# The loop over the attention slots written out in every engine's program

## The reference, cut to what matters

```python
x = x + xattn(layernorm(x), ctx, ctx, mask, Wq, bq, Wk, bk, Wv, bv, Wo, bo)   # 16 heads of 8
x = x + ffn(layernorm(x), Wr, W1, b1, W2, b2)                                 # 8 experts, top 2

# xattn: q = qn @ Wq + bq, k = c @ Wk + bk, v = c @ Wv + bv, per head
score = q @ k.T / sqrt(8); attn = softmax(score); out = (attn @ v) @ Wo + bo
# ffn: probs = softmax(x @ Wr.T); each token goes to its best two experts
h = gelu(x @ W1[e] + b1[e]); y = h @ W2[e] + b2[e]
```

## Time and profile before

| what | value |
|---|---|
| median of three runs | 1009.66 us (1009.06 to 1009.77) |
| the profiled execution, its own time | 1012.47 us |
| its span, first to last instruction | 1010.7 us |
| mean granted TensorE clock | 0.915 |
| PE / DVE / ACT / POOL busy | 81% / 70% / 54% / 49% |
| instructions in the trace | 22541 |

### The profile page before, as it was taken

How to read it: one execution, slowest core, us unless ns; L and a number is a source line. 1 busy time by engine, 2 the same in 40 slices (tenths; PEclk the granted TensorE clock), 3 DMA queues, 4 the chain that set the end, 5 groups by cost and what they waited for, 6 DMA issues and landing times.

```text
span 1010.7 us, 22541 instructions
## 1 busy us (share of the span) xinstructions
PE 822.4 (81%) x5927; PEld 595.5 (59%) x5927; DVE 706.6 (70%) x2191; ACT 550.4 (54%) x1005; POOL 492.9 (49%) x672
## 2 busy tenths in 40 slices
PE   3887899879879978979978988851999999999900
PEld 2555565656556556656655655630888888888700
DVE  6645778767868868868768877643577777777736
ACT  5534455545545545544545554331888888888700
POOL 5333444435434534534534455354177777767730
PEclk9778899989989999989999998885899999999955
DMA  5444443223323323422323344465877777777249
GB/s 152 104 115 116 125 135 95 69 69 96 81 63 99 89 63 79 101 71 67 96 68 83 91 113 116 115 242 175 261 236 240 247 247 243 236 244 247 86 142 356
DMA packets 136613, 143.34 MB, mean 142 GB/s; under 512 B 19884, under 2 KB 101143, under 8 KB 135512
## 3 DMA queue, kind: packets, MB, share of 16 engines
q1 hardware_dynamic: 117672, 119.18, 42.0%
q0 software_dynamic: 9088, 17.07, 4.8%
q10 hardware_dynamic: 9776, 6.29, 2.0%
HBM read 72.61 MB, written 36.08 MB: 108 GB/s over the span
## 4 chain that ended last, share of the span: by engine, by line
PE 49%; DVE 19%; issue 13%; DMA 9%; SPq 5%; POOL 3%; ACT 2%; DVEq 1%; POOLq 0%; ACTq 0%
DVE mx L677 7%; PE bank L1231 5%; PE bank L1405 4%; PE bank L1407 3%; PE bank L1243 3%; PE bank L1406 3%; PE bank L1393 3%; PE bank L1390 3%; PE bank L1391 3%; PE bank L1221 3%; DMA kb<-ks 3%; DMA qb<-negm 3%; DVE yy L687 3%; DMA qb<-yd 2%; PE bank L1179 2%
## 5 line engine op out<-in xcount | busy, mean ns | idle before, releaser
L607 POOL DMA_INDIRECT yd<-vs,idt x156 | 164.6, 1055 | 85.7 <-DVE vs L973 45.9
L1038 ACT ACTIVATE pt<-bank 120x512 f32<-120x512 f32 x256 | 145.6, 596 | 92.4 <-PE bank L1231 90.7
L677 DVE TENSOR_REDUCE mx<-bank 128x4 f32<-128x480 f32 x256 | 159.9, 647 | 37.6 <-PE bank L1221 37.6
L522 POOL DMA_INDIRECT xd<-rows,posi x128 | 129.1, 1009 | 110.0 <-DVE posi L752 64.3
L953 DVE TENSOR_TENSOR qb<-hid,qb 128x512 fp32r<-128x512 f32 x156 | 109.5, 702 | 71.0 <-ACT hid L1130 69.7
L1221 PE MATMUL bank<-kb,qs 128*128 128x480 f32 x256 | 104.5, 454 | 41.0 <-DVE mx L677 22.0
L1231 PE MATMUL bank<-qb,ks 128*120 128x512 f32 x256 | 124.3, 507 | 7.4 <-DMA qb<-negm 7.2
L1127 ACT ACTIVATE qb<-bank,btile 128x512 fp32r<-128x512 f32 x156 | 107.6, 690 | 34.0 <-PE bank L1407 25.7
L1243 PE MATMUL bank<-pt,vs 120*32 120x128 f32 x2048 | 113.8, 296 | 5.1 <-ACT pt L1038 4.2
L1130 ACT ACTIVATE hid<-bank,btile 128x512 f32<-128x512 f32 x156 | 106.3, 682 | 0.0
L1221 PEld LDWEIGHTS bank<-kb,qs 128*128 128x128 f32 x256 | 48.7, 200 | 82.0 <-DVE mx L677 56.9
(11 more groups left out here) (200 smaller groups left out, 2101.2 us busy)
## 6 DMA issues: line engine op xcount, KB each, us to landing
kb<-wd SPq DMA_DIRECT2D x40, 512.0 KB, 5.2
qb<-wd SPq DMA_DIRECT2D x38, 512.0 KB, 5.0
qb<-qs SPq DMA_DIRECT2D x128, 128.0 KB
kb<-ks SPq DMA_DIRECT2D x128, 120.0 KB
rows<-xd SPq DMA_DIRECT2D x39, 264.0 KB, 2.8
wd<-wsp SPq DMA_DIRECT2D x8, 1024.0 KB, 5.3
qb<-yd SPq DMA_DIRECT2D x16, 512.0 KB, 5.6
xd<-zrows SPq DMA_DIRECT2D x8, 528.0 KB, 3.7
```

The source lines that it names most:

```text
L522: g.indirect_dma_start(xd, bass.IndirectOffsetOnAxis(ap=posi[r.phase][:, bk:bk + 1], axis=0), rows[r.phase][:, bk // 2, bk % 2, :], None, ...
L607: g.indirect_dma_start(yd, bass.IndirectOffsetOnAxis(ap=idt[k][:, j:j + 1], axis=0), yrow[p.parity][:, j, :], None, bounds_check=2 * NTOK ...
L677: v.tensor_reduce(mx[:, b, gg, :], wide[(4 + u) % 3][:, 0:J * KL].rearrange("p (j k) -> p j k", j=J), op=ALU.max, axis=AX.X).then_inc(w_fr ...
L1038: a.activation(pt[t % NP][:].rearrange("p j q -> p (j q)"), scores[t % 2][0:KL, :], ACT.Exp, scale=SCALE).then_inc(exp_done, 1)
```

## The change

The loop goes away; all slots are written out in every engine's program, with their numbers as constants.

```diff
         def slots(eng, body):
 
-            for s in range(-2, 4):
-                body(At(s // 4, s % 4), s)
-            with eng.Fori(1, NCH // 4 - 1) as quad:
-                for phase in range(4):
-                    body(At(quad, phase), None)
-            for s in range(NCH - 4, NCH + 2):
+            for s in range(-2, NCH + 2):
                 body(At(s // 4, s % 4), s)
```

## The result

The changed kernel was run four times: 976.2, 981.4, 984.6 and 1964.6 us. The ratio of the mean times of the other three and of the kernel before (1009.7 us) is 0.971 (95% interval 0.966 to 0.977). Five later runs, in a session in which the kernel before takes 1008.7, have a median of 977.3: 0.969 (0.967 to 0.971). The kernel before repeats within about 2 us there; the changed one spreads over 8 (972.0 to 980.5), which the forecast did not have.

The account below looks back on a forecast made before the run. The loop's five branches back, with DVE's instruction-fetch stalls, were taken as dear: 31.1 us. Gains 31.1 + 5.3 + 1.7 less fetches 3.7 gave 34.4, so 1009.66 - 34.4 = 975.3 us, range 969.9 to 982.3.

Parts of the forecast that it names:

- first rival: Only DVE's stalls go; POOL's and SP's tenths are taken up elsewhere, slots stay at 18.18: 982.3 us, chance 0.25.
- Step 1: Five branches back in the 24 loop slots go on every engine, gaining 31.1 us, of which the branches themselves 30.5.
- the two stalls: DVE's 2.51 and 2.35 us at each branch back: fetches of the branch's target and the block behind it.
- 1.9 us for each branch: Rest of each branch's 6.78 us beyond DVE's stalls, put down to PE's clock at its lower level afterwards.
- Step 3: Register instructions go in the 24 slots: gain 5.3 us from POOL and 1.7 from SP, nothing on DVE, ACT, PE.
- POOL's 0.22: POOL's L555 ends 0.22 us earlier per slot, releasing DVE's yy sooner: 5.3 us over 24 slots, bounds 0 and 5.3.
- SP's: SP issues L364 0.14 us earlier per slot, 3.4 us in all; half taken, 1.7, bounds 0 and 3.4.
- The length forecast for yy: Sign of being right: DVE's yy takes 0.98 us instead of 1.20 once POOL's L555 ends earlier.
- Step 2: Instruction blocks fetched in order throughout cost 3.7 us: the first iteration's 0.6 over six groups of slots; bounds 0 and 7.4.
- second rival: Fetching in order costs more, two or three half-microsecond delays per four slots: 9.6 us, time 985 to 988, chance 0.08.
- Step 4: Queues, slots -2 to 3 and 28 to 33, expert tiles and the end: no DMA moved or added, counted 0.
- slower rival: Every block costs its fetch, stopping PE 2.4 us at about 32 block edges: 77 us, time 1049, chance 0.03.

Follow-up runs that it names:

- the first profile: Profiled execution of the changed kernel, all engines written out, in its first session: 984.6 us, 440.0 us for the 24 slots.
- the three later ones: Profiles of the unedited changed kernel in later sessions: 436.8, 433.0 and 432.2 us for the 24 slots; ratios 0.968, 0.962 and 0.969.
- the second run: The changed kernel again, no edit, for its spread: ratio 0.968 (0.960 to 0.975) to the kernel before, 436.8 us for the 24 slots.

## Why the prediction was right, and where it was not

**The direction and the cause** were right. Of the 27.9 us of span that went, 27.4 are in the loop's slots. Both medians, 981.4 of the first three runs and 977.3 of the later five, lie inside the range of 969.9 to 982.3, 6.1 and 2.0 us above the forecast of 975.3. The first one does so by luck: the fetches cost more than their upper bound, and the registers' 2.1 us above the forecast kept the sum inside. It is also chance that 27.4 is just what the first rival had (31.1 - 3.7): its condition, slots that stay at 18.18, did not come.

**Step 1, the branches (31.1 us).** Right in size, place and engine: both "issue" waits of DVE left, and DVE's program alone gives back 28.8 us of the 24 slots. The reading of the two stalls as target and next block was right too, and the second could be taken away by itself. The term included 1.9 us for each branch from PE at its lower clock, and that also went.

**Step 3, the registers (7.0 us).** Measured 24 x (18.18 - 17.80) = 9.1. POOL's 0.22 was right as it stood. SP's was halved for fear of ACT's copy of onT; it counted in full in three slots of four. The first rival, that these tenths would be taken up elsewhere, did not happen. The length forecast for yy was off by SP's share: yy is 0.84 to 0.85 us long in a plain slot and not 0.98, since POOL's rest now ends 0.37 us earlier in the slot, its own 0.22 and SP's 0.15.

**Step 2, the fetches (3.7 us, at most 7.4).** This is the term that failed. Taken as all that the 24 slots last beyond 24 x 17.80, it measured 12.8 us in the first profile, and 9.6, 5.8 and 5.0 in the three later ones. With PE's loop kept, 2.2 to 2.9 us of this are still there, so the meetings with PE's blocks are worth some 2 to 10 us. Part of the rest looks like the same with q14's smaller blocks: in all four profiles slots 15, 20 and 24 have a packet of q14 1.7 to 2.4 us after their start, and take 0.1 to 0.4 us more than a plain one. No run moved these. The mechanism was the one named, a block that shares the DMA engines with negm's small DMA. The sizing was wrong: I took 0.6 us from one iteration and multiplied it by six. That iteration held one meeting, in slot 7, of a cheap kind. In the written-out program PE's blocks come some 15 us apart in slots of 17.8, so their place in the slot wanders, and every fifth slot or so (7, 13, 18, 23 and 28) one lands on the DMA. A meeting costs 0.6 to 3.3 us, and its price has a step:

```profile
290.20:293.20 3.00, 2.76 (x18) 2.09 (x17) 1.84 (x13) 1.02 (x2) 0.67 (x1) 0.57 0.76 174
...
181.00:184.00 3.00, 2.77 (x29) 2.04 (x29) 2.28 (x16) 1.20 (x3) 0.50 (x2) 1.00 0.69 170
```

These windows of the changed kernel are just after the late DMA in slot 13 and in slot 7. In slot 13 PE's scores by key came 1.9 us late and the granted clock was 0.57 behind it, so that the slot lost 3.3 us. In slot 7 they came 1.0 late, the clock stayed at 1.00, and the slot lost 1.0. The wait is about as long as the q8 packet itself takes: over the 16 meetings in slots 7, 13, 18 and 23 of the four profiles the packets took 0.9 to 1.6 us and the scores came 0.6 to 1.9 us late. The fall of the clock adds 1.4 to 1.5 us to it.

The number of these falls is most of what differs between the profiles. In slots 4 to 27 the clock fell four times in the first, twice in the second, and never in the third and fourth, which had 12.8, 9.6, 5.8 and 5.0 us. With some 1.45 us off for each fall, 7.0, 6.7, 5.8 and 5.0 are left. That should be one reason for the changed kernel's spread of 8 us as well; the other runs were not profiled. It isn't the only one: with PE's loop kept the runs still spread over 5.7 us, and the slots ahead of slot 4 ended between 120.2 and 124.8 us in these profiles.

Slot 25 lost 2.0 us in the first profile by a meeting of another kind, with the blocks of kb that the prediction had named beside negm. The chain there, and a window behind it:

```profile
513.74 4.22 DMA kb<-ks
...
519.40:522.40 3.00, 3.00 (x14) 1.65 (x14) 2.01 (x7) 1.50 (x3) 0.61 (x1) 0.50 0.46 110
```

A packet of q8 and one of q14 come 8.6 and 9.2 us into the slot, while that DMA runs, and behind it the clock is at its lower level. In the three later profiles both packets are there too, the clock stays at 1.00, and the slot loses 0.4. With PE's loop kept, or with PE's blocks cut elsewhere, it takes 17.8.

The second rival, that fetching in order costs a little more, had 9.6 us for this term, nearer to 12.8 and 9.6 than the forecast was, but by two or three small delays in each group of four slots; the runs show fewer and dearer ones. The lower end of its time, 985, adds the 9.6 to the forecast, which has 3.7 for the same thing already; in place of these it gives 981.2.

The three terms are all cut out of the same 24 slots, so they add up by the way they are defined: 31.1 + 9.1 - 12.8 = 27.4.

**Step 4** counted the rest at 0. In the first profile slot 28 was 1.1 us longer than before (22.40 for 21.29), with its own q8 packet 1.3 us into it; in the expert stage a window of 238.2 us holds the same 1188 matmuls in both kernels. The slower rival, each block costing its fetch, did not come: of the blocks on q8 in slots 4 to 27 of the first profile, only those in slots 7, 13, 18, 23 and 25 left a slot above 18.2 us.

**Open.** Why the clock fell in some meetings and not in others is not shown: the length of PE's wait does not decide it (see the last section). The run of 1964.6 us was not followed. No run looked at single DMA engines during a meeting; that the block delays the DMA is shown by timing and by moving it, not by watching the queue.

## What to carry to other kernels

When an engine fetches its loop's body anew in each iteration, as DVE did here and PE, ACT, POOL and SP did not, its branch back costs a fetch, and if the loop starts just ahead of a block's edge it costs two. Look at "issue" waits behind the loop's line engine by engine: write out only the program that stalls there, or move the loop's start by a few instructions, and leave the others in their loops. A program written out is not free: its blocks travel with the data, and a small DMA that the chain waits for pays when they meet. Also ask of each gain in a plain slot whether it holds in the others: POOL alone written out made the slots after a branch longer.

## What the runs showed of the hardware that was not expected

- A DMA of 16 KB that starts with one packet of instructions of 16 KB on q8 took up to 4.07 us instead of 2.35.
- A loop on DVE that leaves 428 instructions in the trace for each iteration (228 of the engine, 200 of its sequencer) is fetched again in each iteration, in blocks of 8 KB. PE's body, with over 1300 (584 matmuls, as many weight loads, 145 of the sequencer), is kept: q8 brought nothing in the 406 us of the earlier trace rows.
- The length of a wait does not say whether PE's clock falls to its lower level behind it. In the first profile PE stood idle for 1.09 us at the meeting in slot 23 and for 1.19 in slot 18, and the clock fell. In slot 7 of the second it stood idle for 1.15, and in slot 11 of the kernel with PE's blocks cut elsewhere for 1.34, and the clock stayed at 1.00. A fall made the slot 1.4 to 1.5 us longer on top of the wait: slot 7 of the second run lost 1.17 us, just the wait, and slot 18 lost 2.98 for a wait 1.54 longer.
